# Expert output product turned round: five one-pass products of split operands in place of four full-precision ones

## The chip, the cores and the metric

One core of one Trainium2 chip runs the whole model, batch 8. The metric is the device time of one launch in microseconds, as the median of several runs. TensorE (PE) multiplies, VectorE (DVE), ScalarE (ACT) and GpSimd (POOL) work beside it, and SyncE (SP) issues most transfers.

## The reference

Eight images (3x112x112) and eight texts (128x192) become 178 rows of 192 features each. One attention block follows, then a mixture of experts, cut here to what the change touches:

```python
scores = softmax(xt @ gate_w + gate_b)            # T = 1424 rows, 16 experts
# best 4 of 8 pairs by scores + bias, in them the best 4 experts
w_full = scores * 2.5 where chosen, else 0        # T x 16
up  = silu(einsum('td,edh->teh', xt, Wu) + bu)    # d = 192, h = 128
gt  = einsum('td,edh->teh', xt, Wg) + bg
act = up * gt * w_full[:, :, None]
y = einsum('teh,ehd->td', act, Wd) + w_full @ bd
sh = silu(xt @ sWu + sbu) * (xt @ sWg + sbg)      # shared expert
h = h + y + sh @ sWd + sbd
```

All is float32.

## The kernel before

Every engine has one program written out by hand; they meet in counting semaphores (`then_inc`, `wait_ge`), and each engine keeps to its own order.

**Attention.** The batches go in four pairs, each pair in six steps of four heads. While PE works, GpSimd sums the embedding table by accumulating transfers. The last pair's output projection (`project`) fills PE until about 259 us, and group 0's features, gate and routing are laid among it.

**Expert stage.** The rows lie in 12 tiles of 128 or 100 rows, in three groups of four tiles (`NG = 3`, `GT = 4`); a group is `WIDE[g]` = 484, 484 or 456 rows wide. A group takes `STEPS = 17` steps, the shared expert and then the 16 others, so step n = 17 g + e. `up_gate(n)` makes, with hidden features on the partitions and the group's rows as columns, five one-pass products (type float32r) into bank n % 2 and five into bank 2 + n % 2: W and x are each split into a rounded high part and a remainder, and the products high x high, high x low and low x high are summed (`products`, lines 886 to 890; the 64 rows over 128 of W and x are stacked). ACT makes the silu (line 588), DVE multiplies it with the row of gate weights (`weigh`, line 1121) and fuses gate, bias and silu into `hidT` (`fuse`, line 1134). `down(n)` then multiplies with Wd: for each of the four tiles `hidT` is the stationary operand (128 x up to 128) and Wd the moving one (192 columns), in full float32, accumulated in banks 4 and 5 with the rows on the partitions (line 919). In the profile each such matmul is two entries, so a step shows eight. `down_biases(g)` adds the experts' biases in the same way, once a group (line 913). PE's order is

```python
up_gate(0)
for g in range(NG):
    for k in range(STEPS):
        up_gate(n + 1)
        # k == 3, 4, 5, 13: turn_a, turn_b, gate, turn_rows of group g + 1
        if k == 0:
            down_biases(g)
        down(n)
```

so that `down(n)` follows the up and gate products of the next step. At a group's end `finish(g)` on DVE adds banks 4 and 5 to the residual R, tile by tile (line 1142), and a transfer takes it out, for the last group from SP and ACT (line 648).

**Beside it.** In group 0 every expert's W is split once: ACT rounds it (`w_high`, lines 577 and 580), POOL makes the remainder (`w_low`, line 467), DVE stacks the rest (`w_stack`, line 1112), three experts ahead. POOL also makes the remainders of the next group's x (`x_low_a`, `x_low_b`, lines 456 and 462) and the reciprocal square roots (`rstd`, line 423). The next group's features, gate, routing and weights are spread over the steps of the present one: `experts_in` in steps 1 and 2, exponentials on ACT after step 7, routing on DVE in steps 8 to 12. The gate weights are turned into rows (`turn_rows`, line 784; `rows_out`, line 572), written by SP to HBM (line 351) and read back broadcast over all partitions, one row an expert, in a ring of four buffers (line 357).

## Time and profile before

| what | value |
|---|---|
| median of 3 runs | 451.04 us (450.31 to 451.21) |
| profiled execution, its own time | 450.73 us |
| profiled execution, span of the records | 448.9 us |
| PE, DVE, ACT, POOL busy | 436.1, 276.2, 187.3, 68.5 us |

The span is what the records cover; the execution's own time has 1.8 us more around it. Busy time is the union of an engine's instructions. Matmuls are pipelined: the printed length of one is longer than its distance to the next, so that a series is measured from start to start. PEld is the loading of stationary operands, which runs beside the products.

### The profile page before, as it was taken

To read this page: it belongs to the slowest core of one execution; us is meant where nothing else is said; L and a number is where in the kernel's file an instruction comes from. 1 tells how busy PE (TensorE), PEld (TensorE's weight loads), DVE (VectorE), ACT (ScalarE), POOL (GpSimd) and SP (SyncE) were. 2 spreads that over 40 slices of the span, in tenths; PEclk is the share of its full clock that TensorE was granted. 3 is DMA by queue.
4 is the path that set the end of the run, shared out by engine and by line. 5 is a ranking of instruction groups with operands and counts; after the bars stand their busy time and mean duration, and the time that the engine had idled before them with its cause. 6 is when DMAs were issued, how large, how long until landed. Compare 5 with 4: busy or idle time off the path is not lost.

```text
span 448.9 us, 7171 instructions
## 1 busy us (share of the span) xinstructions
PE 436.1 (97%) x2570; PEld 379.1 (84%) x2570; DVE 276.2 (62%) x917; ACT 187.3 (42%) x565; POOL 68.5 (15%) x91
## 2 busy tenths in 40 slices
PE   8699999999999999999999999999999999999996
PEld 8488769977699766997778999999999999999995
DVE  4588966378664896538958755488563475433433
ACT  1476668245682366923542055543113412112111
POOL 3113221232122312210003213231002000000000
PEclk9799999999999999999989999999999999999999
DMA  8967999999999999997550043221232221332210
GB/s 209 271 262 132 213 214 213 213 213 213 214 214 213 214 212 214 213 213 193 180 169 1 1 167 111 67 66 46 91 81 66 68 67 55 99 66 73 64 42 35
DMA packets 20997, 63.61 MB, mean 142 GB/s; under 512 B 2572, under 2 KB 10836, under 8 KB 20578
## 3 DMA queue, kind: packets, MB, share of 16 engines
q0 software_dynamic: 7552, 39.39, 41.5%
q1 hardware_dynamic: 12546, 22.78, 17.5%
q10 hardware_dynamic: 864, 1.00, 0.9%
q8 instruction: 20, 0.33, 0.3%
q14 instruction: 15, 0.12, 0.1%
HBM read 61.88 MB, written 1.27 MB: 141 GB/s over the span
## 4 chain that ended last, share of the span: by engine, by line
PE 62%; DMA 26%; DVE 6%; issue 2%; ACT 1%; POOL 1%; SPq 0%; DVEq 0%; POOLq 0%
DMA area_w<-in_L_attn_wte_dram 25%; PE bank L919 15%; PE bank L802 7%; PE bank L890 5%; PE bank L889 5%; PE bank L887 5%; PE bank L888 5%; PE bank L886 5%; PE bank L751 2%; PE bank L693 2%; DMA hin<-L_tok_cls_embedding_dram 1%; PE bank L699 1%; PE bank L695 1%; POOL rs L423 1%; PE bank L742 1%
## 5 line engine op out<-in xcount | busy, mean ns | idle before, releaser
L802 PE MATMUL bank<-woT,area_o 128*128 128x192 f32 (+1 forms) x432 | 72.3, 327 | 0.0
L802 PEld LDWEIGHTS bank<-woT,area_o 128*128 128x128 f32 (+1 forms) x432 | 69.8, 182 | 0.6 <-issue 0.6
L515 ACT ACTIVATE pm<-pm,nmax 128x128 f32<-128x128 f32 x96 | 37.4, 391 | 74.1 <-DVE nmax L1024 74.1
L1121 DVE TENSOR_TENSOR area_b<-area_b,area_w 128x484 f32<-128x484 f32 (+1 forms) x36 | 24.1, 669 | 51.6 <-ACT area_b L588 50.1
L430 POOL DMA_DIRECT2D area_w<-in_L_attn_wte_dram x26 | 31.2, 1216 | 127.2 <-DMA area_w<-in_L_attn_wte_dram 127.2
L588 ACT ACTIVATE area_b<-bank,area_k 128x484 f32<-128x484 f32 (+1 forms) x24 | 15.8, 657 | 59.8 <-PE bank L890 59.7
L751 PE MATMUL bank<-pT,xn 128*128 128x356 f32 x96 | 39.7, 495 | 0.0
L538 ACT ACTIVATE area_b<-xb,w 64x192 f32<-64x192 f32 x96 | 38.2, 444 | 0.8
L886 PE MATMUL bank<-area_w_r,area_o_r 128*128 128x484 f32 (+1 forms) x84 | 37.3, 445 | 0.0
L919 PE MATMUL bank<-area_k,area_b 128*128 128x192 f32 (+1 forms) x192 | 35.3, 326 | 0.0
L1022 DVE CUSTOM_DVE_ANT_0 pm<-bank,cmask 128x128 f32<-128x128 f32 x96 | 24.0, 286 | 16.4 <-PE bank L703 16.1
L919 PEld LDWEIGHTS bank<-area_k,area_b 128*128 128x128 f32 (+1 forms) x192 | 31.6, 182 | 0.9
L887 PE MATMUL bank<-area_w_r,area_o_r 128*128 128x484 f32 (+1 forms) x84 | 31.7, 377 | 0.0
L693 PE MATMUL bank<-area_a,xa 128*128 128x256 f32 x96 | 30.0, 395 | 0.3 <-ACT area_b L538 0.3
L588 ACT ACTIVATE area_b<-bank,area_a 128x484 f32<-128x484 f32 (+1 forms) x18 | 11.8, 658 | 40.3 <-PE bank L890 40.3
L752 PEld LDWEIGHTS bank<-pT,xn 128*128 128x128 f32 x96 | 18.2, 190 | 10.5
L919 PE MATMUL bank<-area_a,area_b 128*128 128x192 f32 (+1 forms) x144 | 26.3, 325 | 0.0
L1012 DVE TENSOR_TENSOR area_a<-xa,w 128x768 f32<-128x768 f32 x24 | 22.1, 952 | 4.5 <-ACT xb L507 4.4
L919 PEld LDWEIGHTS bank<-area_a,area_b 128*128 128x128 f32 (+1 forms) x144 | 23.9, 181 | 1.0
L1134 DVE SCALAR_TENSOR_TENSOR area_b<-bank,area_k,area_b 128x484 f32<-128x484 f32 (+1 forms) x24 | 17.1, 712 | 9.8 <-PE bank L890 4.7
L695 PE MATMUL bank<-xa,area_a 128*128 128x178 f32 x96 | 23.0, 322 | 0.0
L742 PE MATMUL bank<-pT,xn 128*64 128x356 f32 x96 | 20.3, 501 | 2.5 <-ACT pT L524 2.5
(214 smaller groups left out, 916.4 us busy)
## 6 DMA issues: line engine op xcount, KB each, us to landing
area_w<-in_L_attn_wte_dram POOLq DMA_DIRECT2D x28, 1344.0 KB, 12.6
area_w<-gate_rows SPq DMA_DIRECT2D x24, 242.0 KB, 3.1
area_k<-in_experts_dram SPq DMA_DIRECT2D x8, 353.0 KB, 5.3
area_w<-gate_rows SPq DMA_DIRECT2D x12, 228.0 KB, 3.2
area_a<-in_experts_dram SPq DMA_DIRECT2D x6, 353.0 KB, 5.2
area_b<-gate_rows SPq DMA_DIRECT2D x8, 242.0 KB, 3.1
woT<-in_L_attn_W_o_dram SPq DMA_DIRECT2D x1, 1728.0 KB, 15.0
area_o<-in_x_dram SPq DMA_DIRECT2D x4, 384.0 KB, 8.6
```

Of the source, the lines that this page charges most:

```text
L430: pool.dma_start(wacc[:, side], wte_v[c], accum_op=ALU.add, max_dma_last_dim=4 * WR * E // 2).then_inc(wte_in[side], 16)
L515: act.activation(pm[:, sl, n, :], pm[:, sl, n, :], ACT.Exp, scale=-1.0, bias=nmax[:, sl, n:n + 1], accum_out=psums[:, sl, n:n + 1])
L538: last = act.activation(qb[side, b, :, h, :], xb[side, b, :].rearrange("p (c t) -> p c t", c=3), ACT.Copy, scale=w2b[side, h:h + 1])
L588: act.activation(sil[:, sl, 0:w], bank[sl][:, 0:w], ACT.Silu, bias=bcol(e, 0)).then_inc(silu_ready, 1)
L693: pe.matmul(splits[k], xa[:, b, 0:P], qa[:, b, 0:2, at, :].rearrange("p c j t -> p j c t"), start=True, stop=False, skip_group_check=True)
L695: pe.matmul(SIDE_TAIL[k], qa[:, b, 2, at, :].rearrange("p j t -> p (j t)"), xa[:, b, 0:S], start=False, stop=False, skip_group_check=True)
L742: pe.matmul(o, xn[:, b, 0, P:E], pT0[:, jj:GRP:2, :], start=True, stop=True)
L751: pe.matmul(o, xn[:, b, 0, 0:P], pT0[:, 2 * q:2 * q + 2, :], start=True, stop=True)
L802: last = pe.matmul(o, oT[:, c, at:at + n], woT[:, c, :], start=(c == 0), stop=(c == NCH - 1))
L886: pe.matmul(o, high, xah[:, p, 0:w], start=True, stop=False)
L887: pe.matmul(o, high, xal[:, p, 0:w], start=False, stop=False)
L919: last = pe.matmul(summed(j, rows_), hidT[:, sl, at:at + rows_], wdn(e), start=False, stop=(e == STEPS - 1), skip_group_check=True)
```

## The change

The output product is transposed. Wd becomes the stationary operand and the hidden features the moving one, with the group's rows as columns, in float32r. Both are split. ACT rounds Wd (`down_high`) and the hidden product (`hidden_high`), POOL makes the remainders (`down_low`, `hidden_low`; the very last one DVE). Of the 192 output features 128 go to bank 4 (Wd high x hidden high, Wd low x hidden high, Wd high x hidden low). The last 64 go to bank 5, with the high part of Wd in the first 64 stationary columns and the low part in the other 64, times hidden high and hidden low. The three products with hidden high (`down_high(n)`) run in the step after the gate product of step n + 1, the two with hidden low (`down_low(n)`) a step later still. The old `hidT` in two buffers becomes one of three (`HELD = 3`), with as many for the rounded part. The biases become two products over 81 rows (weights thrice: high part, high part against the low part of the biases, low part). At a group's end ACT copies bank 4 and DVE bank 5 to SBUF, PE turns them back by eight transposes into banks 6 and 7 (`turn_back`), and DVE adds them to R, two tiles at a time, the last 64 features in two additions. The preparation of the next group moves a step later. In the memory plan `woT`, `wtok`, `pm`, `pt` and `pT0` move into areas that are used again for the new operands.

```diff
+    EARLY = 4
+    HELD = 3
+    WSUM = 81
...
@@ sync
-                sp.wait_ge(wT_ready, g + 1)
-                sp.dma_start(rows[g, :, 0:WIDE[g]], wT[0:NE, g % 2, 0:WIDE[g]]).then_inc(wrow_out, 16)
+                sp.wait_ge(wT_ready, 2 * g + 1)
+                sp.dma_start(rows[g, :, 0:WIDE[g]], wT[0:NE, 0:WIDE[g]]).then_inc(wrow_out, 16)
...
-            sp.wait_ge(out_read, NT - 1)
-            sp.dma_start(out[:, NT - GT:NT - 1, :], R[:, NT - GT:NT - 1, :]).then_inc(last_out, 16)
+            sp.wait_ge(out_read, 2 * NG - 1)
+            sp.dma_start(out[:, NT - GT:NT - 2, :], R[:, NT - GT:NT - 2, :]).then_inc(last_out, 16)
@@ gpsimd
+            def down_low(e):
+                pool.wait_ge(wdh_ready, e + 1)
+                pool.tensor_tensor(wdh(e)[:, E:2 * P], wd(e)[:, P:E], wdh(e)[:, P:E].bitcast(F32), ALU.subtract).then_inc(wdl_ready, 1)
+                pool.tensor_tensor(wda_low(e), wd(e)[:, 0:P], wdh(e)[:, 0:P].bitcast(F32), ALU.subtract).then_inc(wdl_ready, 1)
+            def hidden_low(n):
+                sl, w = n % HELD, WIDE[n // STEPS]
+                pool.wait_ge(hid_high_ready, n + 1)
+                pool.tensor_tensor(hid_low[:, sl, 0:w], hidT[:, sl, 0:w], hid_high[:, sl, 0:w].bitcast(F32),
+                                   ALU.subtract).then_inc(hid_low_ready, 1)
+            w_low(0)
+            w_low(1)
+            down_low(0)
+            down_low(1)
             rstd(GT, PAIRS + 1)
...
                 for k in range(STEPS):
+                    if STEPS * g + k + 1 < STEPS * NG:
+                        hidden_low(STEPS * g + k)
+                    if g and k == 3:
+                        pool.wait_ge(out_read, 2 * g)
+                        pool.dma_start(out[:, GT * (g - 1):GT * g, :], R[:, GT * (g - 1):GT * g, :]).then_inc(out_done, 16)
                     if g == 0 and k + WAH0 < NW:
                         w_low(k + WAH0)
+                    if g == 0 and k + EARLY < NW:
+                        down_low(k + EARLY)
@@ scalar
+                act.activation(wT[0:WSUM, 0:w], bank[7][0:WSUM, 0:w], ACT.Copy).then_inc(wT_ready, 1)
+                act.activation(wTr[0:WSUM, 0:w], bank[7][0:WSUM, 0:w], ACT.Copy).then_inc(wT_ready, 1)
...
+            def hidden_high(n):
+                sl, w = n % HELD, WIDE[n // STEPS]
+                act.wait_ge(hid_ready, n + 1)
+                act.activation(hid_high[:, sl, 0:w], hidT[:, sl, 0:w], ACT.Copy).then_inc(hid_high_ready, 1)
...
                     if g == 0 and k + WAH0 < NW:
                         w_high(k + WAH0)
+                    if g == 0 and k + EARLY < NW:
+                        down_high(k + EARLY)
...
+                    hidden_high(STEPS * g + k)
+                    if g and k == 1:
+                        summed_out(g - 1)
@@ tensor
+            def down_high(n):
+                pe.wait_ge(hid_high_ready, n + 1)
+                if first and g == 0:
+                    pe.wait_ge(proj_read, 3 * PAIRS)
+                elif first:
+                    pe.wait_ge(summed_act, g)
+                    pe.wait_ge(summed_dve, g)
+                pe.matmul(bank[4][:, 0:w], wdh(e)[:, 0:P], h, start=first, stop=False, skip_group_check=True)
+                pe.matmul(bank[5][:, 0:w], wdh(e)[:, P:2 * P], h, start=first, stop=False, skip_group_check=True)
+                pe.matmul(bank[4][:, 0:w], wda_low(e), h, start=False, stop=False, skip_group_check=True)
+            def down_low(n):
+                pe.wait_ge(hid_low_ready, n + 1)
+                pe.matmul(bank[4][:, 0:w], wdh(e)[:, 0:P], h, start=False, stop=last, skip_group_check=True)
+                pe.matmul(bank[5][:, 0:w], wdh(e)[:, P:2 * P], h, start=False, stop=last,
+                          skip_group_check=True).then_inc(down_done, 1)
...
+                        up(n + 1)
+                    if n >= 2:
+                        down_low(n - 2)
+                    if n + 1 < STEPS * NG:
+                        gate_of(n + 1)
...
+                    if n:
+                        down_high(n - 1)
+                    if k == 2:
+                        if g:
+                            turn_back(g - 1)
                         down_biases(g)
-                    down(n)
+            down_low(STEPS * NG - 2)
+            down_high(STEPS * NG - 1)
+            down_low(STEPS * NG - 1)
+            turn_back(NG - 1)
@@ vector
             def finish(g):
-                dve.wait_ge(down_done, STEPS * (g + 1))
-                for j, (_, n) in enumerate(GROUP[g]):
-                    tile = R[0:n, GT * g + j, :]
-                    dve.tensor_tensor(tile, summed(j, n), tile, ALU.add).then_inc(out_read, 1)
+                for half in range(2):
+                    dve.wait_ge(turned_back, 2 * g + half + 1)
+                    tiles = R[:, GT * g + 2 * half:GT * g + 2 * half + 2, :]
+                    link(dve.tensor_tensor(tiles, back(half)[:, :, 0:E], tiles, ALU.add))
+                    dve.tensor_tensor(tiles[:, :, P:E], back(half)[:, :, E:2 * P], tiles[:, :, P:E], ALU.add).then_inc(out_read, 1)
...
+                    if k == 1 and g:
+                        summed_out(g - 1)
+                    if k == 2 and g:
                         finish(g - 1)
```

## Rows read from the trace of the kernel before

**Rows 1.** The page: busy time by engine; granted TensorE clock in 40 slices.

```profile
PE 436.1 (97%) x2570; PEld 379.1 (84%) x2570; DVE 276.2 (62%) x917; ACT 187.3 (42%) x565; POOL 68.5 (15%) x91
...
PEclk9799999999999999999989999999999999999999
```

**Rows 2.** Chain that ended last, group 2's end: start us, us, what.

```profile
439.04 1.30 PE bank L919 x8
440.55 0.21 PE bank L887
...
442.42 2.71 PE bank L919 x16
```

**Rows 3.** Waits from 255 us on: who waited for whom, us in total, times, longest.

```profile
PEld bank L919 <- DVE area_b L1134: 0.2, 1, 0.2
```

**Rows 4.** Timeline of PE in group 0: start us, us, line, operation.

```profile
263.41 1.46 PE L913 MATMUL bank<-bdx,area_b 128*128 128x192 f32 x8
...
268.20 1.46 PE L919 MATMUL bank<-area_k,area_b 128*128 128x192 f32 x8
...
269.72 0.38 PE L887 MATMUL bank<-area_w_r,area_o_r 128*128 128x484 f32 x1
...
271.70 1.46 PE L919 MATMUL bank<-area_k,area_b 128*128 128x192 f32 x8
...
279.12 0.58 PE L768 MATMUL bank<-ident,hin 128*128 128x128 f32 x4
279.54 1.47 PE L919 MATMUL bank<-area_k,area_b 128*128 128x192 f32 x8
...
283.04 0.29 PE L776 MATMUL bank<-gwa,area_b 128*128 128x16 f32 x2
...
284.64 1.55 PE L919 MATMUL bank<-area_k,area_b 128*128 128x192 f32 x8
```

**Rows 5.** Windows: busy time of each engine over 262 to 321 us.

```profile
262.00:321.00 59.00, 59.00 (x320) 53.79 (x319) 41.01 (x112) 26.14 (x53) 15.39 (x17) 1.00 0.33 99
```

**Rows 6.** Groups of ACT by form, 250 us on: busy us, mean ns.

```profile
L588 ACT ACTIVATE area_b<-bank,area_k 128x484 f32<-128x484 f32 x16 | 10.6, 664 | 36.6 <-PE bank L890 36.6
...
L580 ACT ACTIVATE wbt<-area_a,sign 128x256 fp32r<-128x256 f32 x6 | 3.0, 498 | 0.0
L566 ACT ACT_TABLE_LOAD x2 | 2.6, 1283 | 0.0
...
L577 ACT ACTIVATE area_o_r<-area_a 128x256 fp32r<-128x256 f32 x6 | 2.4, 408 | 0.0
...
L562 ACT ACTIVATE area_w_r<-bank 128x484 fp32r<-128x484 f32 x1 | 0.6, 569 | 0.0
```

**Rows 7.** Timeline of DVE in group 0, three steps.

```profile
264.90 0.66 DVE L1121 TENSOR_TENSOR area_b<-area_b,area_w 128x484 f32<-128x484 f32 x1 [1.28 <-DMA area_w<-gate_rows]
...
302.38 1.22 DVE L1121 TENSOR_TENSOR area_b<-area_b,area_w 128x484 f32<-128x484 f32 x1
...
310.82 0.72 DVE L1134 SCALAR_TENSOR_TENSOR area_b<-bank,area_a,area_b 128x484 f32<-128x484 f32 x1
311.46 0.48 DVE L1112 SCALAR_TENSOR_TENSOR area_o_r<-area_o,upper,wbt 128x256 fp32r<-128x256 f32 x1
```

**Rows 8.** Timeline of the end, all engines.

```profile
445.15 1.15 DVE L1142 TENSOR_TENSOR R<-bank,R 100x192 f32<-100x192 f32 x4 [1.64 <-PE bank L919]
...
446.33 0.35 ACTq L648 DMA_DIRECT2D out_dram<-R  x1
```

**Rows 9.** Timeline of SP: the gate rows' write to HBM.

```profile
259.80 0.34 SPq L351 DMA_DIRECT2D gate_rows<-area_b  x1
```

**Rows 10.** Timeline of POOL in group 0.

```profile
262.70 0.64 POOL L467 TENSOR_TENSOR area_k_r<-area_k,area_o_r 128x256 fp32r<-128x256 f32 x1 [12.47 <-ACT area_o_r L577]
...
280.85 1.23 POOL L462 TENSOR_TENSOR area_w_r<-area_b,area_w_r 128x484 fp32r<-128x484 f32 x1 [0.69 <-ACT area_w_r L562]
...
302.35 0.73 POOL L467 TENSOR_TENSOR area_o_r<-area_o,area_o_r 128x256 fp32r<-128x256 f32 x1 [2.69 <-ACT area_o_r L577]
```

More of the change, by code:

```diff
@@ L629, in _ @@
             w_high(2)
+            down_high(2)
             exps_of_gates(0)
+            down_high(3)
+            act.wait_ge(s_small2, 80)
+            act.activation(bdr[:], bdx[:], ACT.Copy).then_inc(bd_high, 1)
             rows_out(0)
@@ new lines, in down_biases @@
+            def down_biases(g):
+                w = WIDE[g]
+                if g == 0:
+                    pe.wait_ge(bd_ready, 1)
+                pe.wait_ge(wT_ready, 2 * g + 2)
+                pe.wait_ge(wT_low, g + 1)
+                pe.matmul(bank[4][:, 0:w], bdr[0:WSUM, 0:P], wTr[0:WSUM, 0:w], start=False, stop=False, skip_group_check=True)
+                pe.matmul(bank[5][0:64, 0:w], bdr[0:WSUM, P:E], wTr[0:WSUM, 0:w], start=False, stop=False,
+                          skip_group_check=True).then_inc(biases_in, 1)
@@ new lines, in turn_back @@
+            def turn_back(g):
+                pe.wait_ge(wT_ready, 2 * min(g + 2, NG))
+                pe.wait_ge(summed_act, g + 1)
+                pe.wait_ge(summed_dve, g + 1)
+                for j, (at, _) in enumerate(GROUP[g]):
+                    o = summed_back(j)
+                    pe.transpose(o[:, 0:P], summed_a[:, at:at + P], ident[:])
+                    last = pe.transpose(o[:, P:2 * P], summed_b[:, at:at + P], ident[:])
+                    if j % 2:
+                        last.then_inc(turned_back, 1)
@@ L1425 @@
     given['bdown'] = _np.zeros((P, 192), _np.float32)
-    given['bdown'][0:17] = _np.concatenate([ffn['bd'], ffn['sbd'][None]])
+    for part in range(3):
+        given['bdown'][32 * part:32 * part + 17] = _np.concatenate([ffn['bd'], ffn['sbd'][None]])
     given['L0_ffn_gate_w'] = _np.concatenate([ffn['gate_w'], _np.zeros((64, 16), _np.float32)])
```

189 lines of the change are left out of this document (121 added, 68 removed).

## The prediction

> **What bounds the kernel now.** I read the page first: PE is busy 97% of the span, no other engine over 62%, and the granted clock is 9 tenths or more in nearly every slice from mid-span on, the upper of its two levels, 2.4 GHz [rows 1]. The change touches the expert stage, from about 259 us to the end, so only that stage counts. The chain that ended last is there an unbroken run of PE work: eight passes of the down product take 1.30 us, and nine of the one-pass products from 440.55 to 442.42 us take 1.87, that is 0.208 us each at 456 columns [rows 2]. The waits say the same: from 255 us on TensorE's matmuls wait for nobody and its weight loads wait 0.2 us, once [rows 3]. The timeline of one step of group 0 gives the other width: down product at 268.20, the second of ten one-pass products at 269.72, the next down product at 271.70; nine products in 1.98 us are 0.22 us each at 484 columns, and the step is 3.50 us = 10 x 0.22 + 1.30 [rows 4]. (A matmul's printed 0.38 us is pipelined; starts are what to subtract.) Over 262 to 321 us PE is busy all 59 us, DVE 41, ACT 26, POOL 15 [rows 5]. So a PE microsecond removed here is a microsecond of the span, until another engine takes its place; POOL and DVE are the candidates.
>
> **The part that is removed and its substitute.** The old down product is 4 matmuls in 8 passes, 1.30 us per expert step, whatever the group's width. The new one is five one-pass products of 484 or 456 columns, the same kind as the ten of up and gate. No row shows them on these operands; I price them like their nearest kin, 5 x 0.22 = 1.10 and 5 x 0.208 = 1.04 us, with banks 4 and 5 taken in turn. I find nothing that would make one cheaper than its columns; 0.26 us each would eat the whole gain of a step, and no one-pass product in the steady stretch is near that.
> Up to the end of the last gate product, before does 34 down products in groups 0 and 1 and 15 in group 2; after does 34 and, being a step later, 14. Groups 0 and 1: 34 x (1.30 - 1.10) = 6.8 us. Group 2: 15 x 1.30 - 14 x 1.04 = 4.9 us. Together 11.7 us off.
> The bias products are 8 passes a group, of the same form as a down product, so 3 x 1.30 = 3.9 us [rows 4]; they become two one-pass products a group, 4 x 0.22 + 2 x 0.208 = 1.3. That is 2.6 us off.
> The sums are turned back by 8 transposes a group. Four transposes take 0.42 us (279.12 to 279.54) [rows 4], so 0.84 a group; groups 0 and 1 lie on PE's path: 1.7 us on. The rows' transposes yield 96 rows in place of 17 with the same moving columns: nothing.
> Sum up to the last gate product: -11.7 - 2.6 + 1.7 = -12.6 us.
>
> **The tail gets longer.** Before, 442.42 us is the end of the last gate product and the span ends at 448.9: 6.5 us. After, from that same point: the fused product 0.7, its rounding on ACT 0.6 (nearest row: 0.57 for 484 columns [rows 6]), while PE works off ten products (2.1) and the three high ones (0.62, to 2.7); DVE's remainder is ready near 2.1; two low products to 3.1, plus 0.2 of pipeline; the copies of banks 4 and 5 side by side, 0.6, to 3.95; four transposes to 4.55, eight to 5.0; the two additions of a half are 384 and 128 columns, between 0.72 for 484 [rows 7] and 0.29 for 192 (four in 1.15 [rows 8]), so 0.9 a half, to 5.45 and 6.35. From the last addition (446.30) to the span's end before are 2.6 us [rows 8]; the last transfer now holds two tiles, not one, which I leave in those 2.6. That makes 8.95, so the tail costs 2.5 us more (1.5 to 3.5).
> Net of what PE's path shows: -12.6 + 2.5 = -10.1 us.
>
> **What is added beside PE, and its cover.** ACT gets a hidden rounding each step and, in group 0, a rounding of Wd: 0.66 + 0.41 + 0.50 + 0.41 + 0.57 = 2.55 us of a step of 3.30 [rows 6]. The new coupling is that ACT now waits for the fused product of step k before the silu of k+1, and the product of k+1 waits for that silu: silu 0.66, weighting 0.66, fusing 0.72, rounding 0.57 and four handovers of some 0.05 make 2.8 us, under 3.30. The exponentials with their two table loads of 1.28 us put ACT some 2 us behind once a group; PE asks for a silu two steps later and for a hidden product two steps later, so that it has over 4 us of cover. If that cover were gone each load would cost its 1.28. The down product of step n is now asked for some 6.6 us after its gate product, so that the old short wait (0.2 us) goes; what is late next is the copy of banks 4 and 5. At a group's start the first high product waits for both copies: the last low product ends 2.4 us into a step (3 + 5 + 2 products at 0.22, 0.2 of pipeline), the copy takes 0.57 on ACT and at most the 0.72 of the fused product on DVE, and the high product is due at 3.30. That is hidden with 0.2 to spare (0 to 0.5 us, twice). Behind the copy on ACT stands the silu of the next step, behind DVE's the addition, both with microseconds of room. In step 2 of a group DVE waits for the transposes while weighting and fusing of step 3 queue behind it: ready about 1.2 us ahead of the gate product that needs it. The gate rows are written by SP a step later; the write was issued at 259.80 [rows 9] and the first weighting ran at 264.90 [rows 7], 5.1 us, and over two steps (6.6 us) remain. On POOL the reciprocal square root for group 0 now stands behind two W remainders and the four small ones of two Wd, at most 6 x 0.64 = 3.8 us of work on weights that ACT rounds in steps 3 and 4 of the last pair, while the root is wanted only after the pair's last step; without that cover the stage would begin up to 3.8 us later. The output's transfer on POOL moves to step 3; nobody waits for it before the end.
>
> **POOL in group 0 is where I expect to lose.** A lap of its queue is now: remainder of the hidden product, 484 columns, 1.23; remainder of W, 256 columns, 0.64; two remainders of Wd, 64 and 128 columns, which no row shows. In proportion (2.5 ns a column, from both rows) they are 0.16 and 0.32, with a little overhead 0.55; the upper bound is the 256-column row each, 1.28 [rows 10]. That is 2.42 us. And POOL and DVE obstruct each other: the weighting at 302.38 took 1.22 us in place of 0.66 beside a POOL subtraction of 302.35 to 303.08 [rows 7, 10]; it seems to have worked in the 0.52 us after POOL had ended. By the Trainium skill (SBUF — State Buffer, "SBUF: two separate sides") a DVE instruction with two SBUF inputs and a GpSimd one hold the shared ports in turn, each for its whole length; the trace agrees, 1.22 us against 0.66. I count 0.5 for the weighting, 0.27 for the 256-column stacking in proportion (its row is 0.48), 0.2 for handovers: a lap is 3.4 us, beside a PE step of 3.30. By the page's rule alone, with durations uncut, the lap would be 0.66 + 0.48 + 2.42 = 3.56 us and the stall about 2 us more.
> Sum over group 0: up(0) ends 15 products before 263.41, at 260.1; table load 1.28, silu 0.66, W's two roundings 0.91, Wd's 0.41, hidden 0.57 put POOL's first remainder at 263.9. Thirteen laps of 3.4, a last 1.87 (hidden and W), two input remainders 2.5, and 1.5 (an estimate) for the router's and the features' two-input instructions: W's last remainder, of expert 16, is ready at 314.0. PE wants it at: 263.41 + 13 products (266.3) + 17 products, the biases in it (270.0), + 12 x 3.30 + two sets of transposes 0.84 + the gate's own products 1.6 (283.04 to 284.64 [rows 4]) = 312.0. Stall 2.0 us. A lap of 3.25 gives none. With 1.28 for the pair in place of 0.55 the lap is 4.1 and the stall 11.5. I take 2.0, as small subtractions here scale nearly with their columns. Groups 1 and 2 have no W to split: 1.23 of 3.30 us, nothing.
>
> **Sum.** Span 448.9 - 10.1 + 2.0 = 440.8 us. The profiled execution's own time lies 1.8 above its span (450.73), and the median of the runs 0.3 above that (451.04): 442.9 us.
>
> **Rivals.** (a) Likeliest, 45%: PE stays the bound with a stall of 0.5 to 4.5 us in group 0: 441.4 to 445.4, at 2.0 442.9.
> (b) 23%: POOL's laps fit, no stall: 440.9. For it: POOL is quiet for two thirds of its time now, and obstruction happens only where instructions meet. Against: laps of 3.4 beside 3.30.
> (c) 20%: the small subtractions cost 1.0 a pair, lap 3.85, stall 7.8: 448.7; or half of that with DVE late: from 445.5 on. For it: POOL's 256-column row is 0.73 in place of 0.64 where DVE ran beside it, and POOL is made to wait as DVE is.
> (d) The other side, 7%: every POOL instruction has most of its 0.64 as a fixed cost, the lap is 4.1, the stall 11.5: 452.4. It decides from a stall of 10.1 us, a lap of 4.0, in the subtraction of Wd. Against it: 1.23 for 484 columns and 0.64 for 256 leave next to no fixed cost. In this 7% stands 1% for the products not being one-pass on these operands: at over 0.26 us each the change would lose.
> (e) 5%: under 440: the tail costs 1.5 or less and the steps drop more.
> A measurement of this kernel tells 0.2% (0.9 us) from no change: 450.1 to 451.9. Slower by more than that: most of (d), 6%. Same: 2%, its edge and (c)'s. Faster: 92%. The range takes in (a), (b) and all of (c) but its end: 439.8 to 448.5.
>
> **What would show it.** Steps of 3.30 us in group 1 and 3.12 in group 2 (a down product's five at 0.22 and 0.21): right or wrong on the main term. PE idle only in group 0, released by POOL's remainder of W or by DVE behind it; if PE idles at a group's start, the copy of banks 4 and 5 was late. POOL's subtractions of 64 and 128 columns near 0.2 and 0.35: (a) or (b); near 0.6: (d). Last gate product to span's end about 9 us. What would make it wrong: a fixed cost on POOL, ACT and DVE coupled in one loop over 3.3 us in all groups (51 steps x each tenth over = 5 us), or a lower clock in the stage: at the lower level each of its products would double.

## The result, and the profile after

The changed kernel takes 454.84 us (median of 7 runs, 452.39 to 455.93), the kernel before, on the same chips, 450.51 (7 runs, 449.63 to 451.21). The ratio is 1.0089, with a 95% interval of 1.0064 to 1.0114: slower by 0.9%. The prediction, 442.9 us in a range of 439.8 to 448.5, was wrong, and on the wrong side. The profiled execution took 453.21 us, with a span of 451.1.

The page's busy time and granted clock, after; it answers to [rows 1]:

```profile
PE 429.5 (95%) x2423; PEld 361.0 (80%) x2423; DVE 315.3 (70%) x928; ACT 219.3 (49%) x640; POOL 143.6 (32%) x174
...
PEclk9799999999999999999999999999899999999996
```

PE's work shrank by 6.6 us and its share fell by two points, so PE is idle where it was not. DVE has 11 instructions more and is busy 39 us longer. Most of that is not work but instructions that take longer: in e1 below, with the same 928 instructions, DVE is busy 285.0 us, 30 less. POOL's busy time doubled. The clock stayed at its upper level in nearly all slices, the last one excepted.

The waits of the matmuls from 255 us on, after (engine, line, who was waited for, us in total, times, longest; two rows of 0.4 us are left out); it answers to [rows 3], where the only wait was a weight load's, 0.2 us:

```profile
PE bank L866 <- DVE wts L1369: 3.2, 2, 2.5
PE bank L968 <- issue: 2.0, 4, 0.7
PE bank L968 <- DVE area_b L1264: 1.7, 2, 1.5
PE bank L1005 <- ACT area_p_r L636: 1.2, 1, 1.2
PE bank L1005 <- ACT area_p L641: 0.8, 1, 0.8
PE bank L1036 <- DVE area_p L1270: 0.8, 1, 0.8
```

The first three rows lie in group 0, but for 0.7 us of the first, in group 1. The largest, 2.5 us, is the transposing of the gate weights (`wts`), which DVE's routing had not finished. "issue" in the second row is a wait in which the profile names nobody; these four short stalls end at 270.89, 275.40, 305.56 and 311.40 us, each 0.1 us after POOL has ended a remainder of W, and they go away when that remainder comes earlier (below). The third is the fused product, DVE's again. L1005, the high product, waits once for the copy of bank 4 at a group's start and once, in the tail, for the rounded hidden product. The last row, a transpose waiting for its copy, is the end's own: e1 has it too.

To see where the time went I cut each timeline of PE at the first up product of each group and at the first up product of the last step. Lengths in us; the first column is the time at which group 0 starts:

```
                     starts   group 0   group 1   group 2 to    last step
                                                  last step     to span's end
before               258.93   62.35     63.55     55.22          8.85
after                256.15   66.88     61.08     52.10         14.89
```

Group 1 is 2.5 us shorter and group 2 is 3.1 us shorter up to its last step, but group 0 is 4.5 us longer and the tail 6.0. The steps themselves are as forecast, where nothing stalls: 3.28 to 3.31 us in groups 0 and 1 (3.30 forecast), 3.08 to 3.12 in group 2 (3.12 forecast). In group 0, counted from up product to up product, steps 4 to 6 take 12.54 us, 1.8 more than in e1 below, which has the same products, and steps 13 to 15 take 4.30, 5.84 and 7.91 us where e1 takes 3.28, 3.30 and 3.75: 7.7 more. (The last of them holds the transposes of the gate weights.) The earlier start, 2.8 us, isn't the change's: in before's profile the granted clock was 0.58 from 228 to 232 us, in after's 1.00. Over all the kernels below the start goes with that stretch and not with the edit: in the five profiles with a clock of 1.00 there group 0 starts at 256.0 to 257.4 us, in the seven with 0.57 to 0.72 at 257.1 to 259.9. So I compare lengths of stages within the profiles, and medians for the whole.

What the earlier profile didn't have is on DVE. Its timeline in group 0, after (start us, us, line, operation), with POOL's beside it:

```profile
299.37 1.24 DVE L1333 TENSOR_TENSOR tied<-gs,top 128x32 f32<-128x32 f32 x1
...
303.12 1.70 DVE L1343 TENSOR_TENSOR scan<-scan 128x32 f32<-128x32 f32 x3
...
309.47 1.31 DVE L1332 TENSOR_TENSOR scan<-sel,top 128x64 f32<-128x64 f32 x1
...
313.64 2.39 DVE L1343 TENSOR_TENSOR scan<-scan 128x64 f32<-128x64 f32 x4
...
316.85 0.36 DVE L1369 TENSOR_TENSOR wts<-above,sc 128x192 f32<-128x192 f32 x1
```

```profile
299.27 1.29 POOL L510 TENSOR_TENSOR area_b_r<-area_b,area_p_r 128x484 fp32r<-128x484 f32 x1 [2.05 <-ACT area_p_r L636]
...
305.42 0.29 POOL L503 TENSOR_TENSOR area_t_r<-area_o,area_t_r 128x64 fp32r<-128x64 f32 x1
305.68 0.41 POOL L504 TENSOR_TENSOR area_o_r<-area_o,area_t_r 128x128 fp32r<-128x128 f32 x1
...
309.45 1.25 POOL L510 TENSOR_TENSOR area_b_r<-area_b,area_p_r 128x484 fp32r<-128x484 f32 x1 [3.37 <-ACT area_p_r L636]
...
314.05 1.22 POOL L510 TENSOR_TENSOR area_b_r<-area_b,area_p_r 128x484 fp32r<-128x484 f32 x1 [2.05 <-ACT area_p_r L636]
```

Read the two side by side. At 299.37 DVE starts a comparison of 32 columns; POOL has begun its 484-column subtraction at 299.27 and ends at 300.56, and DVE's instruction ends at 300.61. At 309.47 the same: it ends at 310.78, POOL's at 310.70. An instruction of 32 or 64 columns that doesn't meet POOL takes 0.18 to 0.23 us. W's remainder of 256 columns, which follows at once in POOL's queue, holds the next one up too (0.68 us at 300.53, 0.67 at 310.71). The third subtraction, 314.05 to 315.27, lies inside the four scans of 64 columns, which take 2.39 us together; four undisturbed ones take 1.0 (in e1, below). The Wd subtractions that I bounded from both sides are 0.29 and 0.41 us.

Two SBUF inputs are not needed for it. Beside POOL's subtraction of 264.40 to 265.72 us stands an instruction with one tensor input and scalars:

```profile
264.55 1.23 DVE L1234 TENSOR_SCALAR hin<-R,mv,rs 128x64 f32<-128x64 f32 x1
```

Alone it takes 0.30. A fusing, with one of its inputs in PSUM, began at 284.58 in the midst of a subtraction (283.93 to 285.60) and took its usual 0.72 us, and reductions and maxima of a few columns are not held up either.

PE's timeline, after, shows what comes of it, and under it the windows behind its longest wait (window, length, busy us of PE, PEld, DVE, ACT and POOL, granted clock, two columns of DMA):

```profile
305.56 0.46 PE L968 MATMUL bank<-area_w_r,area_o_r 128*128 128x484 f32 x1 [0.67 <-issue]
308.79 0.49 PE L968 MATMUL bank<-area_w_r,area_o_r 128*128 128x484 f32 x1 [1.46 <-DVE area_b L1264]
...
317.26 1.04 PE L866 MATMUL bank<-ident,wts 128*96 128x128 f32 x4 [2.50 <-DVE wts L1369]
...
393.92 0.44 PE L1005 MATMUL bank<-area_p_r,area_e_r 128*128 128x456 f32 x1 [0.84 <-ACT area_p L641]
```

```profile
317.00:318.00 1.00, 0.74 (x5) 0.72 (x5) 0.90 (x3) 0.00 (x0) 0.00 (x0) 0.50 0.00 0
318.00:319.00 1.00, 1.00 (x5) 0.85 (x4) 1.00 (x3) 0.36 (x1) 0.00 (x0) 0.50 0.00 0
319.00:320.00 1.00, 1.00 (x4) 0.85 (x3) 1.00 (x3) 1.00 (x3) 0.68 (x1) 0.50 0.00 0
```

PE had waited 1.46 us once and 2.50 us once within 12 us; then it ran for three us at 0.50, the lower level of 1.2 GHz, so that about 1.5 us of work at the upper level were lost on top of the waits. That is a trait of this profile as much as of the kernel: in e7 and e8 below PE waits 2.39 and 2.32 us at the same place, and the clock stays at 1.00.

### The profile page after: what moved, and what is told of

It reads as the page before. It is cut to its first block and busy times, and to the rows that moved or that the text cites. A ratio compares the mean times of both kernels' runs of the same rounds, so it can differ in the third digit from the quotient of the medians.

```text
span 451.1 us, 7070 instructions
## 1 busy us (share of the span) xinstructions
PE 429.5 (95%) x2423; PEld 361.0 (80%) x2423; DVE 315.3 (70%) x928; ACT 219.3 (49%) x640; POOL 143.6 (32%) x174
## 5 line engine op out<-in xcount | busy, mean ns | idle before, releaser
L510 POOL TENSOR_TENSOR area_b_r<-area_b,area_p_r 128x484 fp32r<-128x484 f32 (+1 forms) x50 | 61.9, 1238 | 101.1 <-ACT area_p_r L636 101.0
L636 ACT ACTIVATE area_p_r<-area_b 128x484 fp32r<-128x484 f32 (+1 forms) x51 | 30.6, 600 | 99.9 <-DVE area_b L1264 99.9
L565 ACT ACTIVATE area_p<-area_p,nmax 128x128 f32<-128x128 f32 x96 | 37.4, 390 | 73.8 <-DVE nmax L1154 73.8
L884 PE MATMUL bank<-area_t,area_o 128*128 128x192 f32 (+1 forms) x432 | 72.3, 327 | 0.0
L884 PEld LDWEIGHTS bank<-area_t,area_o 128*128 128x128 f32 (+1 forms) x432 | 69.8, 182 | 0.6 <-issue 0.6
L832 PE MATMUL bank<-area_p,xn 128*128 128x356 f32 x96 | 39.7, 495 | 0.0
L1152 DVE CUSTOM_DVE_ANT_0 area_p<-bank,cmask 128x128 f32<-128x128 f32 x96 | 24.0, 286 | 16.2 <-PE bank L784 16.0
L968 PEld LDWEIGHTS bank<-area_w_r,area_o_r 128*128 128x128 f32 x84 | 15.9, 189 | 8.9 <-DVE area_b L1264 2.7
L823 PE MATMUL bank<-area_p,xn 128*64 128x356 f32 x96 | 19.7, 487 | 1.8 <-ACT area_p L574 1.7
L776 PEld LDWEIGHTS bank<-xa,area_a 128*128 128x128 f32 x96 | 18.8, 196 | 2.7
L567 ACT ACTIVATE area_p<-area_p,nmax 128x178 f32<-128x178 f32 x48 | 20.6, 428 | 0.0
```

Source lines behind the costliest of these rows:

```text
L510: pool.tensor_tensor(hid_low[:, sl, 0:w], hidT[:, sl, 0:w], hid_high[:, sl, 0:w].bitcast(F32), ALU.subtract).then_inc(hid_low_ready, 1)
L565: act.activation(pm[:, sl, n, :], pm[:, sl, n, :], ACT.Exp, scale=-1.0, bias=nmax[:, sl, n:n + 1], accum_out=psums[:, sl, n:n + 1])
L636: act.activation(hid_high[:, sl, 0:w], hidT[:, sl, 0:w], ACT.Copy).then_inc(hid_high_ready, 1)
L776: pe.matmul(SIDE_TAIL[k], qa[:, b, 2, at, :].rearrange("p j t -> p (j t)"), xa[:, b, 0:S], start=False, stop=False, skip_group_check=True)
L832: pe.matmul(o, xn[:, b, 0, 0:P], pT0[:, 2 * q:2 * q + 2, :], start=True, stop=True)
L884: last = pe.matmul(o, oT[:, c, at:at + n], woT[:, c, :], start=(c == 0), stop=(c == NCH - 1))
```

## The experiments

Three theories stood when the experiments began. One: POOL's subtraction of the hidden remainder obstructs DVE, and DVE is late. Two: POOL's queue itself is late with W's remainder, as I had forecast. Three: the schedule of copies and transposes at a group's start, and the lower clock in the tail, cost the time whatever POOL does. Every edit is one to the changed kernel, except e6. The kernels e1 to e4, e5 to e8, and e9 and e10 ran as three sets, each set on one chip beside runs of before: medians 450.01, 450.0 and 450.02 us. Ratios are to before. The runs of before beside after had 450.51, half a microsecond more, so that a small difference to after has to be read from the ratios and their intervals (after: 1.0089 [1.0064, 1.0114]).

### e1: no hidden remainder on POOL

```
-                    if STEPS * g + k + 1 < STEPS * NG:
-                        hidden_low(STEPS * g + k)
...
-                h, last = hid_low[:, sl, 0:w], e == STEPS - 1
-                pe.wait_ge(hid_low_ready, n + 1)
+                final, last = n == STEPS * NG - 1, e == STEPS - 1
+                h = (hid_low if final else hid_high)[:, sl, 0:w]
+                pe.wait_ge(*((hid_low_ready, 1) if final else (hid_high_ready, n + 1)))
```

The kernel leaves out the product with the hidden remainder: the two low products take the rounded hidden features once more, so that the sum is not the right one while PE does the same work.

> The low products take the rounded hidden features in place of the remainder, so that POOL's 484-column subtraction goes in every step and PE's work stays the same (the output lacks the high x low term; the last step keeps its remainder on DVE). Theory L (POOL's remainder of the hidden product holds up DVE's instructions with two SBUF inputs, and DVE is then late with the routing and the gate weights): from the first up product of group 0 to that of group 1 falls from 66.9 to 57.5 to 59.5 us, groups 1 and 2 lose 1 us each, the weighting is back at 0.66 us, the time is 440 to 443.5. Theory Q (POOL's own queue is late with W's remainder, the step named in the prediction): group 0 falls too, but the weighting's length does not matter and PE's waits on DVE in steps 13 to 15 stay where they come from ACT. Rival K (the new loop silu, weighting, fusing, rounding between ACT and DVE is too long by itself): group 0 stays above 63 us and the time above 448.

Measured: 438.93 us (4 runs, 437.67 to 440.89), ratio 0.9759 [0.9719, 0.98]; span 439.0. PE executes the same 2423 products. After 256 us PE waits once, in the tail:

```profile
PE bank L1035 <- DVE area_p L1269: 0.8, 1, 0.8
```

DVE's groups from 259 us on in e1, and then after's (count, then busy us and mean ns, then idle before them with what ended it):

```profile
L1250 DVE TENSOR_TENSOR area_b<-area_b,area_w 128x484 f32<-128x484 f32 x24 | 16.4, 685 | 16.8 <-ACT area_b L655 15.7 <-DMA area_w<-gate_rows 1.0
L1250 DVE TENSOR_TENSOR area_b<-area_b,area_w 128x456 f32<-128x456 f32 x12 | 7.6, 632 | 15.5 <-ACT area_b L655 15.5
L1342 DVE TENSOR_TENSOR scan<-scan 128x64 f32<-128x64 f32 x8 | 1.8, 223 | 0.2
```

```profile
L1251 DVE TENSOR_TENSOR area_b<-area_b,area_w 128x484 f32<-128x484 f32 x24 | 22.6, 943 | 15.6 <-ACT area_b L657 14.1 <-DMA area_w<-gate_rows 1.3
L1251 DVE TENSOR_TENSOR area_b<-area_b,area_w 128x456 f32<-128x456 f32 x12 | 13.2, 1097 | 12.9 <-ACT area_b L657 12.9
L1343 DVE TENSOR_TENSOR scan<-scan 128x64 f32<-128x64 f32 x8 | 3.2, 397 | 0.2
```

Without the 50 subtractions the weightings fall from 943 and 1097 ns to 685 and 632, the scans from 397 to 223, and the kernel is 15.9 us faster than after (454.84 less 438.93; 14.9 by the two ratios), a little more than any of the three expectations had. By stages e1 beats after by 10.0 us in group 0, 1.0 in each of the other two, and 3.6 in the tail: 15.6. So the loss sits in the subtraction on POOL and in what depends on it, and theory three falls as a theory of its own. e1 alone doesn't tell POOL's queue from POOL's hold on DVE.

### e2, e7: the same subtraction in four pieces, in two

```
-                pool.tensor_tensor(hid_low[:, sl, 0:w], ..., ALU.subtract).then_inc(hid_low_ready, 1)
+                for c in range(4):
+                    part = slice(w // 4 * c, w // 4 * (c + 1))
+                    last = pool.tensor_tensor(hid_low[:, sl, part], ..., ALU.subtract)
+                last.then_inc(hid_low_ready, 1)
```

e7 has 2 in place of 4. The same columns are subtracted, and POOL issues more instructions.

> POOL's remainder of the hidden product in four instructions of 121 (114) columns in place of one. L, with ports held for a whole instruction: a small DVE instruction waits 0.4 us at most in place of 1.2, group 0 falls from 66.9 to 60 to 63 us, the time to 446 to 449. Q: POOL's lap grows by 0.4 us (four of some 0.41 for one of 1.24), group 0 grows by 3 us or more, the time is 455 or more. If the ports were shared by bandwidth and not held, nothing would change for DVE: 453 to 456.

> POOL's remainder of the hidden product in two instructions of 242 (228) columns. L with ports held a whole instruction: waits of 0.6 us, between one piece (454.8) and four (444.9) for DVE; POOL's own length hardly grows (2 x 0.62), so that the sum over both may be the best of the three: 443.5 to 448.

Measured: four pieces 444.92 us (5 runs, 444.43 to 447.61), 0.9905 [0.987, 0.9939]; two pieces 448.04 (10 runs, 445.49 to 451.1), 0.9967 [0.9939, 0.9995]. In four pieces, DVE's groups are

```profile
L1254 DVE TENSOR_TENSOR area_b<-area_b,area_w 128x484 f32<-128x484 f32 x24 | 18.5, 771 | 16.1 <-ACT area_b L660 14.5 <-DMA area_w<-gate_rows 1.4
...
L1346 DVE TENSOR_TENSOR scan<-scan 128x64 f32<-128x64 f32 x8 | 2.3, 281 | 0.2
```

One, two and four pieces: 454.8, 448.0, 444.9 us. The expectations were 446 to 449 for four and 443.5 to 448 for two, so that four did better than I thought. A POOL that is late with its queue would lose by pieces, since each has an overhead (four of 121 columns took 1.65 to 2.50 us together in group 0 of e8, below, against 1.25 for one whole, and in e2 POOL never stands idle from 264.8 to 309.6 us). The kernel gained 9.9 us. So what costs is how long one POOL instruction holds DVE off, not how long POOL works. Groups 1 and 2 and the tail are then those of e1 (60.04, 51.13 and 11.28 us against 60.08, 51.15 and 11.25); what remains is 6.4 us in group 0. There four pieces gain 3.5 us on after, and some 1.5 of them are the stretch at the lower clock, which e2's profile doesn't have; the rest of the gain lies in the later stages.

### e3: copies, transposes and rows a step later

```
-                        if k == 15:          # ACT: rows_out
+                        if k == 16:
...
-                        if k == 14:          # PE: turn_rows
+                        if k == 15:
```

> The transposes of the gate weights move from step 14 to 15 on PE and the rows' copies from 15 to 16 on ACT. If DVE's lateness with the weights is what stalls PE most (317.26 us in the trace, 2.5 us idle and then some 1.7 us at the lower clock): group 0 falls by 3 to 4.5 us, the time to 449 to 451.5. If W's remainder on POOL is the bound at that place, the wait only moves to another row: under 1 us.

Measured: 455.0 us (4 runs, 454.05 to 455.67), 1.0106 [1.0069, 1.0142]: no gain, against an expected 449 to 451.5 if the gate weights alone were late. Waits of PE, e3:

```profile
PE bank L1005 <- ACT area_p L641: 3.5, 2, 1.9
...
PE bank L968 <- DVE area_b L1264: 2.5, 3, 1.5
```

The waits for `wts` are gone, and the wait only changes its place: that for the copy of bank 4 grows from 0.8 us to 3.5. Group 0 is 1.6 us shorter than after's, which is what after lost there at the lower clock; groups 1 and 2 are 1.3 and 0.8 longer.

### e4: products without use in the tail, to keep PE busy

```
+            def stay_warm(count):
+                for _ in range(count):
+                    pe.matmul(bank[0][:, 0:WIDE[NG - 1]], wah(0)[:, 0], xah[:, 0, 0:WIDE[NG - 1]], start=True, stop=True)
...
+            pe.wait_ge(silu_ready, STEPS * NG)
+            stay_warm(5)
...
+            stay_warm(3)
```

> Eight products on data at hand are added in the tail, five ahead of the last three high products and three ahead of the last transposes, into a bank that nobody reads; nothing else changes. If the tail is 3.5 us over the forecast because the granted clock fell to 0.5 after PE had stood idle for 1.2 us: five products go from 0.37 to 0.21 us each, eight transposes from 0.21 to 0.105, with the pipeline's ends 1.5 to 2.5 us off, time 451 to 453. If the clock does not matter: 0 to 0.5 us slower.

The tail in after, timeline of PE, ACT, DVE and POOL:

```profile
436.01 0.58 ACT L636 ACTIVATE area_p_r<-area_b 128x456 fp32r<-128x456 f32 x1 [2.02 <-DVE area_b L1264]
436.50 0.62 ACT L657 ACTIVATE area_b<-bank,area_o 128x456 f32<-128x456 f32 x1
436.67 1.18 POOL L510 TENSOR_TENSOR area_b_r<-area_b,area_p_r 128x456 fp32r<-128x456 f32 x1 [1.97 <-ACT area_p_r L636]
437.16 1.18 DVE L1251 TENSOR_TENSOR area_b<-area_b,area_w 128x456 f32<-128x456 f32 x1 [1.18 <-ACT area_b L657]
438.43 0.69 DVE L1264 SCALAR_TENSOR_TENSOR area_b<-bank,area_o,area_b 128x456 f32<-128x456 f32 x1
439.16 0.59 ACT L636 ACTIVATE area_p_r<-area_b 128x456 fp32r<-128x456 f32 x1 [2.03 <-DVE area_b L1264]
...
442.94 0.59 PE L1005 MATMUL bank<-area_p_r,area_t_r 128*128 128x456 f32 x1 [1.22 <-ACT area_p_r L636]
...
446.10 0.42 PE L1037 MATMUL bank<-ident,area_p 128*128 128x128 f32 x1
```

The same places in e4:

```profile
442.57 1.19 PE L1069 MATMUL bank<-area_w_r,wah_early 128*128 128x456 f32 x5
...
443.93 0.47 PE L1005 MATMUL bank<-area_p_r,area_t_r 128*128 128x456 f32 x1 [0.17 <-ACT area_p_r L636]
...
446.23 0.27 PE L1037 MATMUL bank<-ident,area_p 128*128 128x128 f32 x1
```

And the window 444 to 445 us, in after and in e4:

```profile
444.00:445.00 1.00, 1.00 (x3) 0.37 (x2) 0.00 (x0) 0.00 (x0) 0.00 (x0) 0.50 0.00 0
```

```profile
444.00:445.00 1.00, 1.00 (x5) 0.80 (x6) 0.55 (x1) 0.00 (x0) 0.00 (x0) 1.00 0.00 0
```

Measured: 453.83 us (7 runs, 452.65 to 456.49), 1.0093 [1.0063, 1.0122]: neither of the two expectations, and by the ratios no gain over after's 1.0089. After's clock in the tail was 0.50, behind the 1.22 us in which PE waited; in e4 it is 1.00, 2.4 GHz, and the tail is 13.52 us instead of 14.89. But that the added products did it isn't shown. e10 below has exactly after's tail and none of them; PE waits as long, and the clock stays at 1.00 until 448 us:

```profile
444.08 0.48 PE L1005 MATMUL bank<-area_p_r,area_t_r 128*128 128x456 f32 x1 [1.21 <-ACT area_p_r L636]
```

Its tail is 13.44 us. So the clock is worth some 1.4 us of the tail in a profile in which it falls, and it doesn't fall in each.

The other thing to see in the first of these fences is the loop. ACT rounds at 436.01 and again at 439.16: 3.15 us, made of the rounding 0.58 (the silu behind it starts at 436.50), silu 0.62, weighting 1.18, fusing 0.69 and the handovers. A step of group 2 takes 3.10. The weighting overlaps POOL's 436.67 to 437.85.

### e5: W's remainder ahead of the hidden one in POOL's queue

```
+                    if g == 0 and k + WAH0 < NW:
+                        w_low(k + WAH0)
                     if STEPS * g + k + 1 < STEPS * NG:
                         hidden_low(STEPS * g + k)
...
-                    if g == 0 and k + WAH0 < NW:
-                        w_low(k + WAH0)
```

> In group 0 POOL makes W's remainder ahead of the hidden product's remainder of the same step; the work is the same. Theory Q (POOL's queue order is what makes W late): the waits of up products that end with POOL's W remainder (0.3, 0.8, 0.7, 0.7 and 0.6 us in the trace) go, group 0 falls from 66.9 to 63.5 to 65 us, the time to 450 to 452. Theory L alone (DVE is held up whatever the order): group 0 stays within 1.5 us of 66.9.

Measured: 452.85 us (10 runs, 451.28 to 454.29), 1.0064 [1.004, 1.0089]. Waits of PE, e5:

```profile
PE bank L866 <- DVE wts L1369: 2.6, 2, 2.0
PE bank L968 <- DVE area_b L1264: 2.2, 1, 2.2
```

The four waits with "issue" are gone, and group 0 is 64.55 us in place of 66.88: there was a stall by POOL's queue, as theory two has it, and by the profile it is 2.3 us, by the medians 2.0, by the ratios 1.1 with intervals that overlap (expected were 450 to 452 us). Both profiles have some 3 us at the lower clock in group 0. What is left waits for DVE, and group 1 is 1.4 us longer than after's.

### e6: the subtraction alone, added to the kernel before

```
+        spare = sb("spare", [P, GW])
+        still = sb("still", [P, GW])
...
+            own.mark(pool.memset(still[:], 0.0))
...
+                    pool.wait_ge(hid_ready, STEPS * g + k + 1)
+                    pool.wait_ge(pool_own, own.at)
+                    own.mark(pool.tensor_tensor(spare[:, 0:WIDE[g]], still[:, 0:WIDE[g]], still[:, 0:WIDE[g]], ALU.subtract))
```

Nothing reads the result. There is no loop of ACT and DVE here, and no W or Wd that comes later by it.

> The kernel before with one more POOL subtraction a step, 484 (456) columns of a buffer that nobody else uses, begun when the fused product of the step is done; nothing waits for it. It adds the suspected cost to the kernel before. L: DVE's routing instructions of group 0 and 1 grow by up to 1.2 us where they meet it, and with one step of cover less than after PE waits in group 0: 62.4 grows to 64 to 68 us, the time to 452 to 457. If the loop over ACT is needed for the loss (ACT waits for the fused product only in the kernel after): DVE's instructions grow, but PE does not wait, 449.5 to 451.5.

Measured: 452.22 us (10 runs, 449.79 to 452.76), 1.0048 [1.0023, 1.0073], at the lower end of the 452 to 457 that theory one had. The scans of DVE, in before and in e6:

```profile
L1199 DVE TENSOR_TENSOR scan<-scan 128x64 f32<-128x64 f32 x8 | 1.8, 224 | 0.2
```

```profile
L1205 DVE TENSOR_TENSOR scan<-scan 128x64 f32<-128x64 f32 x8 | 3.7, 460 | 0.2
```

An instruction on POOL that nobody waits for doubles DVE's scans, and group 0 goes from 62.35 to 64.20 us; groups 1 and 2 and the tail stay (63.56, 55.19, 8.90). PE's products in e6 wait 1.0 us for DVE's fused product, where those of before waited for nobody. This is the hold by itself. It costs 2.2 us in a kernel whose step is 3.5 us, and some 15 in the changed one, whose step is 3.3 and whose next silu waits for DVE; how the difference divides between the two was not tested.

### e8: four pieces, and W's remainder first

The edits of e2 and e5 together.

> Four pieces and W's remainder first. After the split group 0 is 63.4 us, 6.5 over the kernel without the hidden remainder (56.9), and PE's waits there end mostly with POOL's W remainder or ACT's roundings. Q in the split kernel: group 0 falls by 2 to 5 us, the time to 440.5 to 443.5. If what is left is DVE's lateness with the gate weights: 444 to 446.

Measured: 444.02 us (4 runs, 442.3 to 445.48), 0.9868 [0.9817, 0.9918]. POOL's timeline and PE's largest wait, e8:

```profile
306.56 2.08 POOL L512 TENSOR_TENSOR area_b_r<-area_b,area_p_r 128x121 fp32r<-128x121 f32 x4
```

```profile
PE bank L869 <- DVE wts L1372: 2.3, 1, 2.3
```

Group 0 is now 60.83 us, from e2's 63.35; e1 has 56.90. By the medians that is 0.9 us less than e2, with intervals that overlap. The kernel beats before by 6.0 us and after by 10.8.

What is left is the hold again. DVE's four scans of 64 columns in e8:

```profile
313.00 1.95 DVE L1346 TENSOR_TENSOR scan<-scan 128x64 f32<-128x64 f32 x4
```

They take 1.0 in e1, and comparisons of 64 columns take 0.48 (310.05 us) in place of 0.22. From the first scan to the end of `wts` DVE works with hardly a gap in both kernels, e8 for 16.5 us and e1 for 12.5: 4.0 us, as much as group 0 is longer. In pieces a lap of POOL's queue takes 3.4 to 3.6 us (306.56 to 310.00, 310.00 to 313.63), more than PE's step of 3.30, so that POOL never stands idle from 264.8 to 315.3 us and DVE always meets it.

### e9, e10: the routing a step earlier

The routing on DVE, five calls in steps 9 to 13 of a group, moved one step ahead: on e8 in e9, on after in e10.

```
-                        if k == 10:
+                        if k == 9:           # first_four(gs, TG)
...
-                        if k == 13:
+                        if k == 12:          # ties, weights_out
```

> Four pieces and W's remainder first, and in addition the routing's last four parts on DVE a step earlier (its first half in step 9 behind the softmax, the weights in step 12), with PE's transposes of the weights still in step 14. In the run without this PE waited 2.3 us for the weights in step 15 and group 0 took 60.8 us. L: the lateness is the same but has 3.3 us more room, that wait goes, group 0 takes 57.5 to 59.5 us, the time is 441 to 443. If DVE's total load in steps 9 to 13 is what counts, the wait moves to a gate product and the time stays at 443.5 to 445.

> The changed kernel with only the routing a step earlier; POOL's remainder in one piece as it was. If cover was all that lacked: the stall before the transposes (2.5 us and 1.7 at the lower clock) goes and group 0 takes 62 to 64 us, the time is 450 to 452. L: DVE stays behind by the same microseconds, PE then waits for a fused product or for W in place of the weights, and group 0 gives back under 2 us: 453 to 455.

Measured: e9 444.65 us (6 runs, 442.94 to 447.16), 0.988 [0.9851, 0.9909]; e10 453.14 (5 runs, 452.94 to 455.71), 1.0093 [1.0063, 1.0124]. Both are as expected if DVE's load counts. No gain over e8, and by the ratios none over after (1.0093 and 1.0089). The profiles agree once the clock is counted: e9's group 0 is 1.4 us longer than e8's and has some 3 us at 0.50 (305 to 308 us), which e8's has not; after's is 1.6 longer than e10's and has them too. In e9 the wait for `wts` is gone, and in its place stands

```profile
PE bank L971 <- DVE area_b L1267: 2.4, 2, 1.8
```

The 2.3 us for the gate weights became 2.4 for the fused product. DVE's work of these steps is late as a whole; which of its results PE meets first depends on the order.

### The stages of all kernels

Cut as above, lengths in us; medians are of the whole kernel. In four of the profiles, after, e4, e5 and e9, the granted clock was 0.50 for some 3 us of group 0, which makes that stage about 1.5 us longer; in the others it was 1.00 from the start of group 0 to its end:

```
                             starts  group 0  group 1  group 2  tail    median
before                       258.93  62.35    63.55    55.22     8.85   450.51
after                        256.15  66.88    61.08    52.10    14.89   454.84
e1  no hidden remainder      259.62  56.90    60.08    51.15    11.25   438.93
e2  four pieces              259.90  63.35    60.04    51.13    11.28   444.92
e7  two pieces               257.06  64.15    60.83    51.12    11.24   448.04
e5  W first                  256.29  64.55    62.48    52.16    13.72   452.85
e8  four pieces, W first     259.88  60.83    60.05    51.12    11.32   444.02
e9  e8, routing earlier      256.01  62.26    60.35    51.13    11.25   444.65
e10 routing earlier          257.17  65.30    62.13    52.86    13.44   453.14
e3  rows later               258.71  65.26    62.40    52.85    14.28   455.00
e4  products in the tail     257.41  66.69    61.10    52.08    13.52   453.83
e6  before, subtraction on   256.65  64.20    63.56    55.19     8.90   452.22
```

## Why the prediction was wrong, point by point

**PE's path and the tail: right.** The sum was -10.1 us before any stall. e1 has all of the change's PE work, copies, transposes and additions, but no obstruction; against before its stages differ by -5.45, -3.47 and -4.07 us, and +2.40 in the tail (forecast +2.5): -10.6 us. The medians say -11.1 (438.93 less 450.01). The five products cost what their kin cost, 0.22 and 0.208 us each. From the end of the last gate product (430.24 us in e1) to the span's end are 8.8 us, where 8.95 were forecast.

**The cover of the pieces beside PE: half right.** In e1, where nothing else is in the way, the exponentials' table loads, the root for group 0, the bias, and the SP and POOL transfers moved a step show in no wait of PE. The copy of banks 4 and 5 I had called "hidden with 0.2 to spare": in after it was late once by 0.8 us (the L1005 row at 393.92), in e1 never. It was the DVE ahead of it that was late, not the copy that was too long; 0.5 twice was my upper bound.

**POOL's lap: its instructions sized right, its stall right by luck.** The hidden remainder is 1.25 us (1.23 forecast), the two Wd subtractions 0.29 and 0.41, 0.70 (0.55 forecast, 1.28 the upper bound). The stalls that e5 removes are POOL's queue, 1.1 to 2.3 us against a forecast 2.0, but not the stall I forecast. I had laps of 3.4 us that pile up until W's last remainder is late. Where POOL's queue ran without a gap a lap took 2.7 to 3.0 us (288.67 to 291.36, 276.25 to 279.21); from 299 us on POOL stood idle 2.05, 3.37 and 2.05 us for ACT's rounding, which waited for DVE; and W's last remainder, ready at 315.96, was 3.3 us ahead of its up product. PE stalled because a remainder of W stood behind the hidden one in the queue, at four places. Rival (d), the fixed cost on POOL, which gave 452.4 us, is refuted by the 0.29 us of the 64-column subtraction, though the time came out on its side.

**The step that failed** is the one in which I said what the obstruction costs: "I count 0.5 for the weighting, 0.27 for the 256-column stacking", and put it to POOL's lap alone. I had priced a meeting of two instructions as a delay of the short one's length on POOL's side. The runs show the other side: a DVE instruction with two SBUF inputs that starts while the 484-column subtraction runs does not end before it, and loses up to 1.1 us even if it has 32 columns. In steps 9 to 13 of group 0 the routing is some twenty small instructions, most of them of that kind. From the first scan of 32 columns to the end of `wts` after takes 18.0 us (299.26 to 317.21), e1 12.5 (299.12 to 311.61): 5.5 us. Counted from the start of group 0, after is already 3.6 us behind where this begins (43.1 against 39.5 us). POOL's order is little of that: e5 has 42.8 there. That is 9.1 of the 10.0 us by which the stage is longer than e1's; the rest falls behind it, where PE lost about 1.5 us at a clock of 0.50. The Trainium skill (SBUF — State Buffer, "SBUF: two separate sides") says that the two engines hold the shared ports in turn, each for its whole instruction; the trace agrees: 1.24 and 1.31 us in place of 0.19 to 0.23 for 32 and 64 columns, while the fusing, which reads one input from PSUM, stayed at 0.72 us. I cited the page and applied it to the lap only, where it made 2 us; on DVE's side it was most of the loss.

**The loop of ACT and DVE: right in form, mis-sized.** "2.8 us, under 3.30" took the weighting at its quiet 0.66. In group 2 it is 1097 ns on average, the loop 3.15 us, and the step to compare it with is group 2's 3.12, not 3.30. The loop is then over the step by a few hundredths, which PE's lead absorbs (the 1.0 us that groups 1 and 2 each lose to e1 are nearly the 0.7 us wait for `wts` in the one and the 0.84 for the copy in the other), but it puts the last hidden product late, so that PE waits 1.2 us in the tail, and in after's profile the clock then fell to 0.50. Together these are 3.6 us of tail (14.89 less 11.25), of which some 1.4 are the clock: e10 has the same wait and no fall, and 13.44 us. I had named the danger ("ACT and DVE coupled in one loop over 3.3 us") and given it no chance.

**The account.** After against e1, by stages: 10.0 in group 0, 1.0, 0.95 and 3.64: 15.6 us. The prediction had 2.0 for all of it. -10.6 + 15.6 is +5.0; less the 2.8 us by which after's group 0 starts earlier in the profile it is the 2.2 by which the spans differ, and beside the 4.3 of the medians.

**What stays open.** e8 keeps 3.9 us of group 0 over e1. e9 shows that the place of the routing isn't what makes them, and the traces that DVE's longer instructions make up that time; a kernel with POOL's work shorter and in pieces at once was not run, nor was the subtraction tried on another engine. Why the clock falls behind one wait of PE and not behind another as long is open, and so is why it fell between 228 and 232 us in seven of the twelve profiles; where it did, group 0 started later.

## What to carry to other kernels

When work goes to POOL, price it on DVE too: each DVE instruction with two SBUF inputs that meets one on POOL can end as late as POOL's does, and here one with a tensor and scalars did so as well (1.23 us for 64 columns); so count the small ones (routing, scans, comparisons), not their columns. If the work must be there, cut it into short instructions; POOL's own time then grows and the kernel can still gain. And a loop over two engines has to be checked with the durations it will have beside the new neighbour, against the shortest step of the kernel and not against the first.

## What the runs showed of the hardware

Splitting one POOL subtraction of 484 columns in four made POOL's part longer (1.65 to 2.50 us for 1.25) and the kernel 9.9 us faster: the hold is per instruction. Held up beside it were instructions with two SBUF inputs and one with a tensor and scalars (1.23 us for 0.30); not held up was the fusing with an input from PSUM (0.72 us). Subtractions on POOL took 0.29, 0.41, 0.64 and 1.25 us for 64, 128, 256 and 484 columns where little was in their way, nearly in proportion, with a little fixed. And in after the clock fell to 0.50 twice where PE had been waiting for others, at 317 and at 443 us; behind waits as long it stayed at 1.00 in e7 and e8 (2.39 and 2.32 us) and, in the tail, in e10 (1.21 us), so that one profile with a fall doesn't make it a trait of the kernel.
